# Eleven tables by matmul, gathered rows for a whole chunk, and embeddings with four samples interleaved, in a recommendation tower on one core

## The reference

```
e = stack([tbl_f[ids[:, f]] for f in range(27)], axis=1)         # 2048 x 27 x 128
z = einsum('bnd,bmd->bnm', e, e), the entries below the diagonal  # 2048 x 351
h = concatenate([z, dense_ctx], axis=1)                           # 2048 x 367
h = maximum(h @ W_top1 + b_top1, 0)                               # 512
h = maximum(h @ W_top2 + b_top2, 0)                               # 256
y = h @ W_top3                                                    # 1
```

## Time and profile before

| | |
|---|---|
| median of 3 runs | 390.16 us (388.52 to 391.35) |
| the profiled execution | 389.1 us, of which 387.3 us are the span from first to last instruction |
| TensorE | busy 87% of the span, mean granted clock 0.96 |
| GpSimd | busy 68% (its 272 indirect DMAs, without the time between them) |
| VectorE, ScalarE | busy 59% and 50% |

### The profile page before, as it was taken

The page is one execution under the profiler, slowest core; times in us unless marked ns, Lnnn a source line. Parts: engine busy times, 40 slices in busy tenths (PEclk is TensorE's granted clock), DMA queues, the critical chain, the costliest instruction groups (busy, mean ns, idle before and its releaser), DMA issues.

```text
span 387.3 us, 15244 instructions
## 1 busy us (share of the span) xinstructions
PE 337.4 (87%) x6096; PEld 304.2 (79%) x6096; DVE 226.7 (59%) x689; ACT 195.1 (50%) x318; POOL 262.9 (68%) x279
## 2 busy tenths in 40 slices
PE   0767699979979999979999997979989996986777
PEld 0656599779969898869989896969988996965765
DVE  4799998548743586438862785438862884411010
ACT  2457446535644465455554664436645554536223
POOL 5777747777777777777777777777777777772000
PEclk9899999989989999999999998999999998996889
DMA  6999542853364326533275328432474327433210
GB/s 180 240 242 258 163 112 54 195 113 105 94 168 105 102 60 164 120 95 95 70 187 121 95 54 203 93 99 76 108 165 102 97 60 195 94 84 80 41 37 0
DMA packets 68596, 45.73 MB, mean 118 GB/s; under 512 B 53478, under 2 KB 56934, under 8 KB 68535
## 3 DMA queue, kind: packets, MB, share of 16 engines
q1 hardware_dynamic: 58237, 26.65, 28.9%
q0 software_dynamic: 8704, 17.84, 18.3%
q10 hardware_dynamic: 1594, 0.31, 0.4%
HBM read 39.02 MB, written 5.76 MB: 116 GB/s over the span
## 4 chain that ended last, share of the span: by engine, by line
PE 62%; DMA 13%; issue 9%; POOL 7%; DVE 4%; ACT 3%; SPq 2%; ACTq 1%; POOLq 0%
PE lookup_ps L508 31%; PE gram_ps L527 10%; PE layer_ps L544 7%; PE gather_ps L493 7%; POOL rows L463 7%; DMA rows<-tbl,index 6%; DMA emb<-tbl 6%; PE layer_ps L556 5%; DVE one_hot L753 2%; PE layer_ps L564 2%; DVE table_lo L760 1%; DMA gram_dram<-gram 1%; ACT emb L620 1%; SPq L344 1%; SPq L389 1%
## 5 line engine op out<-in xcount | busy, mean ns | idle before, releaser
L463 POOL DMA_INDIRECT rows<-tbl,index x272 | 262.1, 964 | 88.5 <-issue 74.8
L753 DVE TENSOR_SCALAR one_hot<-ids_all,row_number 125x256 fp32r<-125x256 int32 x648 | 202.9, 378 | 101.6 <-PE lookup_ps L508 99.1
L508 PE MATMUL lookup_ps<-one_hot,table_hi 125*128 125x256 f32 x640 | 177.9, 310 | 21.9 <-DVE one_hot L753 17.8
L508 PE MATMUL lookup_ps<-one_hot,table_lo 125*128 125x256 f32 x640 | 163.0, 286 | 0.5 <-issue 0.5
L508 PEld LDWEIGHTS lookup_ps<-one_hot,table_hi 125*128 125x128 f32 x640 | 124.6, 195 | 30.7 <-issue 24.1
L508 PEld LDWEIGHTS lookup_ps<-one_hot,table_lo 125*128 125x128 f32 x640 | 125.1, 195 | 0.9 <-issue 0.7
L620 ACT ACTIVATE emb<-gather_ps 128x384 f32<-128x384 f32 (+1 forms) x80 | 86.4, 1080 | 37.7 <-PE gather_ps L493 37.0
L626 ACT ACTIVATE emb<-lookup_ps 128x256 f32<-128x256 f32 x80 | 56.1, 701 | 31.9 <-PE lookup_ps L508 31.8
L527 PE MATMUL gram_ps<-emb 128*26 128x27 f32 x4096 | 59.0, 195 | 11.3 <-issue 8.3
L527 PEld LDWEIGHTS gram_ps<-emb 128*26 128x26 f32 x4096 | 47.9, 107 | 24.3 <-issue 14.1
L493 PE MATMUL gather_ps<-identity,rows 128*128 128x128 f32 x272 | 46.6, 290 | 11.0 <-DMA rows<-tbl,index 10.0
(11 more groups left out here) (36 smaller groups left out, 104.8 us busy)
## 6 DMA issues: line engine op xcount, KB each, us to landing
ids_all<-lookup_ids SPq DMA_DIRECT2D x44, 256.0 KB, 3.4
gram_dram<-gram SPq DMA_DIRECT2D x62, 87.8 KB
emb<-tbl SPq DMA_DIRECT2D x10, 448.0 KB
rows<-tbl,index POOLq DMA_INDIRECT x272
z<-gram_dram SPq DMA_DIRECT2D x14, 117.0 KB
z<-gram_dram SPq DMA_DIRECT2D x7, 91.0 KB
emb<-w SPq DMA_DIRECT2D x3, 192.0 KB
emb<-tbl SPq DMA_DIRECT2D x10, 52.0 KB
```

The costliest lines, as they stand in the source:

```text
L463: pool.indirect_dma_start(rows[g][:, j * DIM:(j + 1) * DIM], None, tables[f], bass.IndirectOffsetOnAxis(index[p][:, h, f:f + 1], 0)).then_ ...
L508: last = nc.tensor.matmul(lookup_ps[k % LOOKUP_BANKS], table[:, k, row, :], one_hot[u % UNIT_RING][:, r, :], start=(row == 0 and table is ...
L753: last = nc.vector.tensor_scalar(one_hot[u % UNIT_RING][:, r, :], table_ids, row_number[0:LOOKUP_PARTS, row:row + 1], None, ALU.is_equal)
```

## The change

Four things are changed together. An eleventh table of 1000 rows is read by matmul (`N_LOOKUP = 11`), so that 16 are gathered; they make four slots of four. The ids come in six parts instead of five, and `EARLY_UNITS` is 28 of now 44 units. `rows` has a buffer and a semaphore for each of the 8 gathers of a chunk (`N_GATHERS`), so that GpSimd can be a whole chunk ahead. `emb` has four samples interleaved: its order is lane, feature, sample of four. A copy of one feature now writes runs of four floats, and a gram product reads its 26 and 27 columns with a step of four floats. Since 11 is odd, the bank of a lookup goes by the chunk's parity too. In the diff, lines without a change are mostly left out.

```diff
...
-N_LOOKUP = 10
+N_LOOKUP = 11
...
-SLOT_SIZES = (4, 4, 3, 3, 3)
+SLOT_SIZES = (4, 4, 4, 4)
...
-ID_PARTS = 5
-TABLES_PER_PART = N_LOOKUP // ID_PARTS
-UNITS_PER_PART = N_UNITS // ID_PARTS
+TABLES_PER_PART = 2
+ID_PARTS = -(-N_LOOKUP // TABLES_PER_PART)
+PART_TABLES = [list(range(N_LOOKUP))[part * TABLES_PER_PART:(part + 1) * TABLES_PER_PART] for part in range(ID_PARTS)]
+UNITS_PER_PART = TABLES_PER_PART * UNITS_PER_TABLE
...
-EARLY_UNITS = 24
+EARLY_UNITS = 28
...
-        rows = [sbuf(f"rows{g}", [P, len(SLOTS[g]) * DIM]) for g in range(len(SLOTS))]
+        rows = [sbuf(f"rows{k}", [P, len(SLOTS[k % len(SLOTS)]) * DIM]) for k in range(N_GATHERS)]
-        ids_all = [sbuf(f"ids_all{part}", [P, TABLES_PER_PART, CHUNK], i32) for part in range(ID_PARTS)]
+        ids_all = [sbuf(f"ids_all{part}", [P, len(PART_TABLES[part]), CHUNK], i32) for part in range(ID_PARTS)]
-        emb = [sbuf(f"emb{p}", [P, CHUNK // PER_TILE, FEATURES, PER_TILE]) for p in range(2)]
+        emb = [sbuf(f"emb{p}", [P, LANE, FEATURES, GROUP]) for p in range(2)]
...
-        rows_in = [semaphore(f"rows_in{g}") for g in range(len(SLOTS))]
+        rows_in = [semaphore(f"rows_in{k}") for k in range(N_GATHERS)]
...
-        ROWS_FREE = len(SLOTS)
+        ROWS_FREE = N_GATHERS
...
             def load_ids(c, part):
-                src = lookup_ids[bass.ds(c, 1), part, :].rearrange("c b -> (c b)")
+                columns = slice(PART_TABLES[part][0] * CHUNK, (PART_TABLES[part][-1] + 1) * CHUNK)
+                src = lookup_ids[bass.ds(c, 1), columns].rearrange("c b -> (c b)")
...
             def prefetch_ids(c, part):
-                sp.wait_ge(unit_ready, (c - 1) * N_UNITS + (part + 1) * UNITS_PER_PART)
+                sp.wait_ge(unit_ready, (c - 1) * N_UNITS + (PART_TABLES[part][-1] + 1) * UNITS_PER_TABLE)
                 settle(sp)
...
                     for j, n in enumerate(SLOTS[g]):
-                            rows[g][:, j * DIM:(j + 1) * DIM], None, tables[f],
-                            bass.IndirectOffsetOnAxis(index[p][:, h, f:f + 1], 0)).then_inc(rows_in[g], 16)
+                            rows[k][:, j * DIM:(j + 1) * DIM], None, tables[f],
+                            bass.IndirectOffsetOnAxis(index[p][:, h, f:f + 1], 0)).then_inc(rows_in[k], 16)
...
                 g = k % len(SLOTS)
-                pe.wait_ge(rows_in[g], (c * HALVES + k // len(SLOTS) + 1) * 16 * len(SLOTS[g]))
+                pe.wait_ge(rows_in[k], (c + 1) * 16 * len(SLOTS[g]))
                 pe.wait_ge(gather_out, c * N_GATHERS + k + 1)
                     last = nc.tensor.transpose(gather_ps[k % GATHER_BANKS][:, j * P:(j + 1) * P],
-                                               rows[g][:, j * DIM:(j + 1) * DIM], identity[:, :])
+                                               rows[k][:, j * DIM:(j + 1) * DIM], identity[:, :])
-            def lookup_unit(c, u):
+            def lookup_unit(c, p, u):
...
-                        last = nc.tensor.matmul(lookup_ps[k % LOOKUP_BANKS], table[:, k, row, :],
+                        last = nc.tensor.matmul(lookup_ps[(p * N_LOOKUP + k) % LOOKUP_BANKS], table[:, k, row, :],
...
                     for tile in range(TILES):
-                        group = emb[p][:, (b * T_PER_BANK + t) * TILES + tile, :, :].rearrange("d f s -> d (f s)")
+                        group = emb[p][:, b * T_PER_BANK + t, :, tile]
...
-                        lookup_unit(c0 + c, k)
+                        lookup_unit(c0 + c, (p0 + c) % 2, k)
...
-                    lookup_unit(c, k)
+                    lookup_unit(c, c, k)
...
-                dst = emb[p][:, h * P // PER_TILE:(h + 1) * P // PER_TILE, n0:n0 + n, :].rearrange("d t f s -> d f t s")
-                src = gather_ps[k % GATHER_BANKS][:, 0:n * P].rearrange("d (f t s) -> d f t s", f=n, s=PER_TILE)
+                dst = emb[p][:, h * HALF_LANE:(h + 1) * HALF_LANE, n0:n0 + n, :].rearrange("d t f s -> d f t s")
+                src = gather_ps[k % GATHER_BANKS][:, 0:n * P].rearrange("d (f t s) -> d f t s", f=n, s=GROUP)
                 nc.scalar.activation(dst, src, ACT.Copy).then_inc(gather_out, 1)
             def copy_lookup(c, p, k):
-                src = lookup_ps[k % LOOKUP_BANKS].rearrange("d (t s) -> d t s", s=PER_TILE)
+                src = lookup_ps[(p * N_LOOKUP + k) % LOOKUP_BANKS].rearrange("d (t s) -> d t s", s=GROUP)
             def split_high(c, k, to, ready, reads):
...
-                                           .reshape(N_CHUNKS + 1, ID_PARTS, TABLES_PER_PART * CHUNK)),
+                                           .reshape(N_CHUNKS + 1, N_LOOKUP * CHUNK)),
```

## The result

| | median | range |
|---|---|---|
| before | 389.89 us | 388.52 to 391.35, 4 runs |
| changed | 397.89 us | 395.99 to 399.2, 4 runs |

What follows compares the result with a forecast made beforehand. GpSimd's gathers were taken to set the pace at 42.6 us a chunk, with TensorE 2.4 us behind. The terms, 11.8 - 10.8 + 3.75 - 2.8 = +1.95 us on 390.16, gave 392.1 us, range 382.5 to 405.

Steps and rivals of the forecast that it cites:

- the case called likeliest: Whole kernel: GpSimd stops being the bound, TensorE takes its place at the same pace; 392.1 us, chance 0.46.
- the rival of half the read rate: Gram products: reads with a step of four run at half rate, +12.3 us, giving 404.4 us; chance 0.22.
- GpSimd stops being the bound, TensorE takes over: Steady chunks: GpSimd's gathers fall from 42.6 to 40.1 us a chunk, below TensorE; chunks still take 42.5 to 43 us.
- TensorE +11.8 us: Lookups by matmul: 16 more matmuls, 1.92 us, less 0.24 for two transposes; net +1.68 a chunk, seven chunks counted.
- The start +3.75: Chunk 0, where VectorE sets the pace: an eleventh table adds its whole 3.75 us.
- The waits for rows, -10.8: TensorE's 7.5 us of waits for gathered rows go, and 3.3 us of lower clock after them.
- ScalarE's copies: Copies of 512 elements fall from 1.24 to 0.66 us; nothing in the steady part, -2.8 us at the end.
- The grams' reads, taken as nothing: Gram products: reading 26 and 27 columns with a step of four floats costs nothing, the low bound.
- the 2.9 ns of cover: Each gram product: 2.9 of 8.7 ns go to something else, so reading may become 1.5 times as slow before it shows.
- the far bound of 14.1: Each gram product: reads slowed 2.4 times, as ScalarE's write with a step of 27, take 14.1 ns.
- The price that I had for such a rate, +22 us: Gram products at ScalarE's ratio: +5.4 ns for each of 4096, +22 us or more, 414 and up; chance 0.10.
- The loop's edges go: TensorE's other waits, 8.1 us, mostly where the loop turns, vanish too, giving 384.0 us; chance 0.22.

Runs made afterwards that it cites:

- experiment 8: The kernel before, ten tables, with a row buffer for each of its ten gathers of a chunk, nothing else: 384.04 us, ratio 0.9883.
- experiment 1: The changed kernel with each gram product reading neighbouring floats instead of every fourth (doesn't compute the reference): 387.15 us, ratio 0.9951.
- experiment 2: The changed kernel with samples not interleaved, layout, copies and reads of `emb` as before; eleven tables and deep rows stay: 388.46 us, ratio 0.9965.
- experiment 4: The kernel before with copies writing runs of four floats and grams reading neighbours (doesn't compute the reference): 389.54 us, ratio 1.0006.
- 5: The changed kernel with neighbouring floats as weights, moving columns still read with a step of four (doesn't compute the reference): 393.3 us, ratio 1.0058.
- 6: The changed kernel with neighbouring floats as moving columns, weights still read with a step of four (doesn't compute the reference): 394.31 us, ratio 1.0118.
- 7: The changed kernel with two samples interleaved instead of four, reads with a step of two, writes in runs of two: 386.04 us, ratio 0.9936.
- experiments 9 to 12: On a slow chip (before 659.69 us): before with deep rows and pairs 665.34; before with eleventh table 594.81; before interleaved by four 652.96; changed kernel unedited 625.84 us.

## Why the prediction came out as it did

The range, 382.5 to 405, holds 397.89, and slower had the largest of my chances. But the case called likeliest, 392.1 and no price for the reads, did not come, and 397.89 lies above its 387 to 396. What came lies between it and the rival of half the read rate, 404.4. The range holds it because it was stretched to that rival, and because several terms came out too dear while one was missing. That is luck in part.

- **GpSimd stops being the bound, TensorE takes over**: right. GpSimd waits for transposes, TensorE waits for no rows. Depth, which I named for it, doesn't bring it about alone: with deep rows and 34 gathers 5.8 of the 7.5 us are left (experiment 8).
- **TensorE +11.8 us**: the chunks came out as forecast, the term too dear. With plain reads (experiment 1) the chunks take 42.6 us each, against 42.9 before and "42.5 to 43" forecast: in the steady part the eleventh table costs what GpSimd's relief gives back. But TensorE is busy for 41.20 us of them on the mean, against 40.47 before, 0.7 more for my 1.68. The transposes alone went from 5.41 to 4.81 us, 0.6 less for my 0.24, in eight groups instead of ten; I had put such switches at nothing. What makes the rest of the difference isn't shown.
- **The start +3.75**: right in size, VectorE's 3.74 us. From deep rows alone to experiment 1 the first layer 1 moves from 112.7 to 119.6 us, 6.9 for a forecast of 3.75 + 2 x 1.68 = 7.1, with two tables' lookups in that stretch.
- **The waits for rows, -10.8**: they are gone from the changed kernel. What I saw and passed over is the 4.0 us wait of GpSimd itself. I read it as an exception in a saturated stretch, when on a saturated engine each stall goes straight to the end. Experiment 8 puts it at 5.4 us, on the kernel before.
- **ScalarE's copies**: sized well (0.60 for 0.66 us), placed badly. The end got 5.6 us shorter for my 2.8, but 3.3 us of that come without short copies (55.0 to 51.7, experiment 2), where the last gather is issued at 329.1 instead of 351.3. What the short copies add there is within the scatter of single traces, and alone they give nothing (experiment 4).
- **The grams' reads, taken as nothing**: the step that failed. I let the 2.9 ns of cover and the small step decide. The product went from 8.7 to (1.07 - 0.22)/63 = 13.5 ns, close to the far bound of 14.1 that came from ScalarE's write. The cover was read off a mean: in the bank of the earlier trace rows the recorded starts are 7.3 ns apart over the first half and 10.1 over the second, so that most of the 2.9 ns were gaps late in the bank and no room in each product. In the changed kernel the starts come in fours, some 54 ns from four to four, from end to end. The price that I had for such a rate, +22 us, was wrong the other way: of (13.49 - 8.73) ns x 4096 = 19.5 us, 7.3 take the place of slow stretches and gaps that plain products had anyway, and 10.7 us arrive in the time.
- **The loop's edges go** (the faster rival): no. TensorE stands still there for nearly as long, 1.6 and 1.8 us for 2.0 and 2.1, and what GpSimd's pace covered is open now: 47.2 and 45.9 us for chunks that otherwise take 43.

The terms without the grams were 4 us too dear together (experiment 1 is 2.1 us below before, my sum was 1.95 above), and the missing term is 10.7. Both numbers hold the time of experiment 1, which drops out of their sum, so that -2.1 + 10.7 = 8.6 comes near the measured 8.0 is no check of its own.

The warning that I weighed and set aside, from the Trainium skill ("Advanced Engine Details and Errata", section "SBUF Cachelines": lines of 16 bytes, at least two accesses on each), is borne out by experiments 1, 5, 6 and 7: a step of four floats slows both reads of TensorE, a step of two does not. The section gives the penalty no size; that it would be the half rate "or worse" was my own step, and 13.5 ns against the 11.7 of that rival came out as worse.

## What to carry to other kernels

Interleave as far as the readers allow: runs of two floats gave ScalarE's copies most of their gain, and at four TensorE's reads paid for it. (Three wasn't tried.) When two engines are bound within 2 us of each other, relieving one buys nothing beyond that and uncovers every cost on the other; the same reads cost 2.6 us before and 10.7 after. On a saturated engine look for its one stall before its work: five more row buffers gave 5.4 us, and the eleventh table on top of them lost 4.4.

## What the runs showed of the hardware

- A fp32 product of 26 by 27 columns, four side by side, starts every 8.7 ns on the mean of the fastest banks of 64, and every 6.6 ns over 16 of them at best; with a step of two floats every 8.7; with a step of four on either operand every 12.7, on both 13.5. Four side by side make 4 x 12.7 = 51 ns for 26 or 27 floats, 1.9 to 2.0 ns each. That is the rate of ScalarE's write with a step of 27 (2.0 ns). That one cause is behind both is a guess.
- ScalarE's copies of 512 elements: 1235 ns with a step of 27, 669 in runs of two, 600 in runs of four.
- On the chip of experiments 9 to 12 the kernel before took 659.7 us where it took 389 on others, and the four kernels traced there had 95 to 157 us of gaps before TensorE's gram products that the profile puts down to issue.
